# Routing choice on the logits, gate weights off GpSimd, the single tile first, and the first units' order, in a mixture-of-experts and time-mix layer

## The reference, cut to what matters

```python
xn = layernorm(x)                                # x: (2, 2048, 256), so 4096 tokens
out = x + attn(xn) + ffn(xn)

# ffn: 8 experts, 2 for each token, and a shared expert
logits = xt @ gate_w.T + gate_b                  # (4096, 8)
scores = softmax(logits)
top_w, top_i = top_k(scores, 2)
gate_dense = sum(one_hot(top_i, 8) * top_w[..., None], axis=1)
h = silu(xt @ w1e.T + b1e) * (xt @ w3e.T + b3e)  # each expert, 256 wide
y = einsum(h @ w2e.T + b2e, gate_dense)
z = silu(xt @ ws1.T + bs1) * (xt @ ws3.T + bs3) @ ws2.T + bs2   # shared, 512 wide

# attn: k, v and r from xn, a scan over time (wkv), then (sigmoid(r) * wkv) @ out_w.T
```

## Time and profile before

| | |
|---|---|
| median of 3 runs | 487.76 us (485.83 to 487.76) |
| the profiled execution | 489.11 us, its span 487.4 us |
| mean granted TensorE clock | 0.951 |
| TensorE busy | 435.8 us (89% of the span) |
| VectorE busy | 382.1 us (78%) |
| ScalarE busy | 227.1 us (47%) |
| GpSimd busy | 265.7 us (55%) |
| route / run_experts / mix, roughly | 0 to 75.5, 75.5 to 274, 274 to 487 us |

### The profile page before, as it was taken

One profiled execution on the slowest core, in us unless ns is written; L12 is line 12 of the kernel. 1 busy time (PEld: TensorE's weight loads), 2 busy tenths in 40 slices (PEclk: granted clock), 3 DMA queues, 4 the chain that ended last, 5 costly groups with the idle time before them and its releaser, 6 DMA issues.

```text
span 487.4 us, 8291 instructions
## 1 busy us (share of the span) xinstructions
PE 435.8 (89%) x2522; PEld 367.0 (75%) x2522; DVE 382.1 (78%) x707; ACT 227.1 (47%) x365; POOL 265.7 (55%) x237
## 2 busy tenths in 40 slices
PE   0896064989999999999999998999999999999997
PEld 0442053778988889888888776989898989898987
DVE  7896996876788698886966478897887969696953
ACT  1445342675876858678485543141323242414131
POOL 5005988746285865859846587837262645445000
PEclk9999555799999999999999998999999999999999
DMA  5879994326567485342454692352626170705001
GB/s 177 259 253 279 304 236 97 96 80 197 209 228 250 120 270 182 133 169 91 154 144 168 213 346 69 113 200 87 195 76 206 36 244 21 258 2 174 11 33 45
DMA packets 46242, 78.27 MB, mean 161 GB/s; under 512 B 5788, under 2 KB 32132, under 8 KB 46204
## 3 DMA queue, kind: packets, MB, share of 16 engines
q1 hardware_dynamic: 37388, 55.85, 33.5%
q0 software_dynamic: 8816, 21.93, 17.4%
HBM read 49.55 MB, written 28.21 MB: 160 GB/s over the span
## 4 chain that ended last, share of the span: by engine, by line
PE 69%; DVE 8%; POOL 8%; issue 6%; DMA 5%; SPq 1%; ACT 1%; POOLq 0%; DVEq 0%; ACTq 0%
PE ps_g L971 15%; PE ps_y L971 7%; PE ps_w L1429 6%; PE ps_w L1431 5%; PE ps_w L1430 5%; PE ps_w L1495 5%; PE ps_w L1496 5%; PE ps_w L1494 5%; DMA w_lo<-w_all 4%; POOL xg L893 3%; PE ps_x L965 3%; PE ps_h L991 2%; POOL w_lo L367 2%; PE ps_v L1429 1%; PE ps_v L1431 1%
## 5 line engine op out<-in xcount | busy, mean ns | idle before, releaser
L893 POOL DMA_INDIRECT xg<-xn_rows,tile_tok x71 | 72.4, 1020 | 30.0 <-issue 17.1
L1398 POOL DMA_INDIRECT yg<-expert_rows,rows x64 | 66.2, 1034 | 23.6 <-issue 17.1
L971 PE MATMUL ps_g<-w_hi,x_hi 128*128 x142 | 57.3, 404 | 2.3 <-DVE w_lo L380 1.7
L971 PE MATMUL ps_g<-w_lo,x_hi 128*128 x142 | 57.0, 402 | 0.0
L971 PE MATMUL ps_g<-w_hi,x_lo 128*128 x142 | 56.8, 400 | 0.0
L1429 PE MATMUL ps_w<-col_hi,s_hi 128*128 128x512 f32 x128 | 50.4, 393 | 0.2 <-DVE shid L1641 0.2
L1431 PE MATMUL ps_w<-col_hi,s_lo 128*128 128x512 f32 x128 | 50.1, 392 | 0.0
L1430 PE MATMUL ps_w<-col_lo,s_hi 128*128 128x512 f32 x128 | 50.1, 392 | 0.0
L1536 ACT ACTIVATE sact<-ps_w,vec_b 128x512 f32<-128x512 f32 x32 | 22.0, 687 | 57.5 <-PE ps_w L1431 57.5
L1406 POOL TENSOR_TENSOR col_lo<-col,col_hi 128x1024 fp32r<-128x1024 f32 x7 | 20.0, 2861 | 49.8 <-ACT col_hi L1518 49.8
L1134 DVE TENSOR_TENSOR hid<-ps_g,act 128x512 f32<-128x512 f32 (+1 forms) x36 | 23.7, 660 | 26.4 <-ACT act L1046 26.2
(11 more groups left out here) (214 smaller groups left out, 1261.6 us busy)
## 6 DMA issues: line engine op xcount, KB each, us to landing
expert_rows<-y SPq DMA_DIRECT2D x35, 256.0 KB, 2.3
w_lo<-w_all SPq DMA_DIRECT2D x16, 384.0 KB, 11.6
table<-mix_tables SPq DMA_DIRECT2D x8, 768.0 KB, 7.5
xin<-x SPq DMA_DIRECT2D x16, 256.0 KB, 3.0
xn_rows<-xn SPq DMA_DIRECT2D x16, 256.0 KB, 3.4
xn_columns<-xT SPq DMA_DIRECT2D x8, 512.0 KB, 3.7
col<-xn_columns SPq DMA_DIRECT2D x8, 512.0 KB, 6.0
res<-x SPq DMA_DIRECT2D x16, 256.0 KB, 3.5
```

What stands on the lines that cost most here:

```text
L893: pool.indirect_dma_start(out=xg[b][:, t, :], out_offset=None, in_=xn_d[:, :], in_offset=bass.IndirectOffsetOnAxis(ap=tile_tok[:, 2 * a + ...
L971: mm = nc.tensor.matmul(out, x[:, k, :], w[:, ds(e, 1), k, cols].rearrange("p o n -> p (o n)"), start=(k == 0 and n == 0), stop=(last and ...
L1398: pool.indirect_dma_start(out=yg[a.buf(2)][:, k, q, :], out_offset=None, in_=y_d[:, :], in_offset=bass.IndirectOffsetOnAxis(ap=picked[a.bu ...
```

## The change

In `choose`, both experts are found on the logits less their maximum, so that the maximum is zero: the first comparison is with zero, the winner is pushed down by -3e38 and the next maximum (`behind`) is found among what is left. `exps` is no longer waited for there. The softmax's sum, reciprocal and product move to a new function `share` that follows each `choose`; the gates are the reciprocal, and exp(behind) times it (ScalarE takes the exponential). `dense` is made by VectorE between the last one-hot batch and `tile_tok`, its rounded copies in `terms` by ScalarE, its low part by VectorE after `tile_tok` and after four `split_lo`.

GpSimd issues ten additions in route. The other six follow gathers 2, 3 and 4 in run_experts, two after each. HIGH and LOW are 10 and 4.

Unit 0 has one tile and all others have two. The order of ScalarE and VectorE in the first units is changed. The low part of `col` is cut by VectorE in the last unit, and in mix the low part of x is cut by VectorE, and the experts' first addition in step 0 is put off to its end.

```diff
-        HIGH, LOW = 12, 1
+        HIGH, LOW = 10, 4
...
             pool.wait_ge(s_xn, NSTEP - 1)
-            for i in range(8):
-                less_first(pool, i)
-
-            pool.wait_ge(s_mask, 3)
-            nc.gpsimd.tensor_tensor(dense[:], score, mask[:].rearrange("p e j -> p j e"), ALU.mult
...
-            for i in range(8, E * KC):
+            for i in range(HIGH):
                 less_first(pool, i)
...
+            act.wait_ge(s_second, 2)
+            nc.scalar.activation(gates[:, 1, :], behind[:], ACT.Exp).then_inc(s_gate, 1)
+            for i in range(HIGH - 2):
+                split(i)
+            act.wait_ge(s_terms, 3)
+            for n in (0, 2):
+                ins = nc.scalar.activation(terms[:, :, n * E:(n + 1) * E].bitcast(F32R), dense[:], ACT.Copy)
+            ins.then_inc(s_terms, 1)
+            for i in range(HIGH - 2, HIGH):
                 split(i)
...
+                own.link(nc.vector.scalar_tensor_tensor(
+                    out=work2[:, t], in0=work[:, t], scalar=0.0,
+                    in1=desc[:, None, :].broadcast_to([P, count, E]), op0=ALU.is_equal, op1=ALU.mult))
+                own.link(nc.vector.tensor_reduce(red[:, t], work2[:, t], AX_X, ALU.max))
+                own.link(nc.vector.tensor_tensor(hot[0][:, t], work2[:, t], wide(red[:, t]), ALU.is_equal))
+                own.link(nc.vector.scalar_tensor_tensor(out=left[:, t], in0=hot[0][:, t], scalar=-3e38,
+                                                        in1=work[:, t], op0=ALU.mult, op1=ALU.add))
+                nc.vector.tensor_reduce(behind[:, t], left[:, t], AX_X, ALU.max).then_inc(s_second, 1)
+                dve.wait_ge(s_second, n + 1)
...
+            def share(n, first_step, last_step):
...
                 dve.wait_ge(s_exp, n + 1)
                 own.link(nc.vector.tensor_reduce(red[:, t], score[:, t], AX_X, ALU.add))
+                own.link(nc.vector.reciprocal(gates[:, 0, t], red[:, t]))
+                own.mark(nc.vector.tensor_tensor(score[:, t], score[:, t],
+                                                 gates[:, 0, t][:, :, None].broadcast_to([P, count, E]), ALU.mult))
...
             choose(0, 0, EARLY)
+            share(0, 0, EARLY)
             for n in range(EARLY, NSTEP):
                 take(At(0, n, NSTEP))
             choose(1, EARLY, NSTEP)
-            for i in range(LOW):
-                split(i)
+            share(1, EARLY, NSTEP)
...
+            dve.wait_ge(s_terms, 2)
+            nc.vector.tensor_tensor(dense[:], score, mask[:].rearrange("p e j -> p j e"), ALU.mult
+                                    ).then_inc(s_terms, 1)
+            dve.wait_ge(s_gate, 1)
+            nc.vector.tensor_tensor(gates[:, 1, :], gates[:, 1, :], gates[:, 0, :], ALU.mult)
             dve.wait_ge(s_hotmm, PAIRS // BATCH)
...
+            for i in range(LOW):
+                split_lo(dve, i)
+            dve.wait_ge(s_terms, 4)
+            nc.vector.tensor_tensor(terms[:, :, E:2 * E], dense[:], terms[:, :, 0:E], ALU.subtract
+                                    ).then_inc(s_terms, 1)
...
-            return min(2, TILES - 2 * a)
+            return 1 if a == 0 else 2
+
+        def first_tile(a):
+            return max(0, 2 * a - 1)
...
             for a in range(AHEAD):
                 gather(a)
+                if 2 <= a < 5:
+                    for i in range(HIGH + 2 * a - 4, HIGH + 2 * a - 2):
+                        less_first(pool, i)
...
-            cut(1, col)
...
-                if a < E // 2:
-                    pe.wait_ge(s_wlo, 2 * KC * (a + 1))
+                if first_tile(a) < E:
+                    pe.wait_ge(s_wlo, KC * min(E, first_tile(a) + tiles(a)))
...
+            cut_x(0)
+            cut_x(1)
+            silu(0)
             split_hi(act, HIGH)
+            cut_x(2)
             split_hi(act, HIGH + 1)
...
                 silu(a + 1)
                 cut_h(a)
                 cut_x(a + 3)
+                if a < 2:
+                    for i in range(HIGH + 2 + 2 * a, HIGH + 4 + 2 * a):
+                        split_hi(act, i)
+                if a == 0:
+                    halves(0)
                 if r == 1 and v < NPIECE:
                     exps(v)
...
             for i in range(LOW, 6):
                 split_lo(dve, i)
             cut_x(0)
+            cut_x(1)
+            hidden(0)
+            grown(0)
+            for i in range(6, 8):
+                split_lo(dve, i)
+            cut_x(2)
+            for i in range(8, 10):
+                split_lo(dve, i)
             differences(0)
...
                 hidden(a + 1)
+                if a == DUOS - 1:
+                    dve.wait_ge(c_whi, 2)
+                    nc.vector.tensor_tensor(col[2][:], col[0][:], col[1][:].bitcast(F32), ALU.subtract
+                                            ).then_inc(c_wlo, 1)
                 cut_h(a)
                 cut_x(a + 3)
-                if a == 0:
-                    for i in range(12, E * KC - 1):
+                if a < 3:
+                    for i in range(10 + 2 * a, 12 + 2 * a):
                         split_lo(dve, i)
-                if a == 1:
-                    split_lo(dve, E * KC - 1)
...
                 if left > 0:
-                    cut(a.plus(1))
                     gather(a.plus(1))
...
+            def cut_x(a):
+                dve.wait_ge(b_xhi, a.i)
+                at_least(dve, b_z, a.i * KS - KS)
+                nc.vector.tensor_tensor(x_lo[a.buf(2)][:], xT[a.buf(2)][:], x_hi[a.buf(2)][:].bitcast(F32),
+                                        ALU.subtract).then_inc(b_xlo, 1)
...
                 if first:
                     hidden(a, 1)
+                    cut_x(a.plus(1))
                 receive(a)
-                if first:
-                    experts(a, 0)
-                elif second:
+                if second:
                     hidden(a, 0)
-                else:
+                elif not first:
                     add_outputs(a.plus(-1))
                 cut_a(a)
+                if left > 0 and not first:
+                    cut_x(a.plus(1))
...
                 if first:
-                    for g in range(1, TOPK * 2):
+                    for g in range(TOPK * 2):
                         experts(a, g)
```

More of the change, by code:

```diff
@@ new lines, in choose @@
+                dve.wait_ge(s_second, n + 1)
+                own.link(nc.vector.tensor_tensor(work2[:, t], left[:, t], wide(behind[:, t]), ALU.is_equal))
+                own.link(nc.vector.tensor_tensor(work2[:, t], work2[:, t],
+                                                 desc[:, None, :].broadcast_to([P, count, E]), ALU.mult))
+                own.link(nc.vector.tensor_reduce(red[:, t], work2[:, t], AX_X, ALU.max))
+                own.link(nc.vector.tensor_tensor(hot[1][:, t], work2[:, t], wide(red[:, t]), ALU.is_equal))
@@ L650, in choose @@
+                nc.vector.tensor_tensor(mask[:].rearrange("p e j -> p j e")[:, t], hot[0][:, t], hot[1][:, t],
+                                        ALU.add).then_inc(s_mask, 1)
+            def share(n, first_step, last_step):
+                t = slice(first_step * Q, last_step * Q)
+                count = (last_step - first_step) * Q
                 dve.wait_ge(s_exp, n + 1)
                 own.link(nc.vector.tensor_reduce(red[:, t], score[:, t], AX_X, ALU.add))
-                own.link(nc.vector.reciprocal(red2[:, t], red[:, t]))
@@ L653, in choose @@
-                own.link(nc.vector.tensor_tensor(score[:, t], score[:, t], wide(red2[:, t]), ALU.mult))
-                cur = score
-                for k in range(TOPK):
-                    own.link(nc.vector.tensor_reduce(gates[:, k, t], cur[:, t], AX_X, ALU.max))
-                    own.link(nc.vector.tensor_tensor(work2[:, t], cur[:, t], wide(gates[:, k, t]), ALU.is_equal))
-                    own.link(nc.vector.tensor_tensor(work2[:, t], work2[:, t],
-                                                     desc[:, None, :].broadcast_to([P, count, E]), ALU.mult))
-                    own.link(nc.vector.tensor_reduce(red[:, t], work2[:, t], AX_X, ALU.max))
-                    own.link(nc.vector.tensor_tensor(hot[k][:, t], work2[:, t], wide(red[:, t]), ALU.is_equal))
-                    if k == 0:
-                        own.link(nc.vector.scalar_tensor_tensor(out=work[:, t], in0=hot[0][:, t], scalar=-2.0,
-                                                                in1=score[:, t], op0=ALU.mult, op1=ALU.add))
-                        cur = work
@@ L762, in run_experts @@
         s_tok, s_xout, s_terms, s_Tout, s_wlo, (HIGH, LOW), route_parts = placed
-        split_hi, split_lo, store_columns = route_parts
+        split_hi, split_lo, store_columns, less_first = route_parts
         raw_vr, col0 = vr[0], col[0]
@@ L960, in turn_x @@
             def turn_x(a):
-                pe.wait_ge(c_gath[a % NG], a // NG * 32 + tiles(a) * 16)
+                pe.wait_ge(c_gath[a % NG], sum(tiles(u) for u in range(a % NG, a + 1, NG)) * 16)
```

(12 more changed lines are left out.)

46 lines of the change are left out of this document (13 added, 33 removed).

## The result

| | before | after |
|---|---|---|
| median of 4 runs each, same chip | 487.53 us (485.83 to 487.76) | 493.99 us (493.19 to 495.31) |
| ratio | | 1.0113, 95% interval [1.0068, 1.0157] |
| profiled execution, its span | 489.11, 487.4 us | 493.19, 491.5 us |
| mean granted clock | 0.951 | 0.948 |
| TensorE / VectorE / GpSimd busy | 435.8 / 382.1 / 265.7 us | 438.6 / 376.7 / 241.0 us |

The forecast was 486.3 us, in 482.5 to 490.2. The kernel is 1.1% slower and lies outside the range. The profiled executions differ by 4.1 us (before's is slower than each of its four runs, after's is the fastest of its four), the medians by 6.5.

The account below looks back on a forecast made before the run. TensorE, 435.8 of 487.4 us busy, loses time in route, from `s_tok` to up(3), and at mix's start. Terms +0.2 + 1.6 + 0.75 - 4.0 = -1.5 us gave 486.3 us, range 482.5 to 490.2.

Parts of the forecast that it names:

- Route: Up to `s_tok`: shorter choice saves 2.8 us, gates without GpSimd's `dense` 2.6 us; `s_tok` at 70.1 instead of 75.51.
- the last rival of C: Route: the long scan isn't GpSimd's doing, `s_tok` 1.8 us later, +0.3 us, 488.1; chance 0.05.
- Up(0) to up(2): First units of run_experts: up(0) at 79.4 instead of 86.73, up(2) at 88.6 after 1.3 us of wait.
- The weights' low parts: First units: TensorE waits for low parts, up(3) at 97.5, up(4) at 106.8; +0.2 us at the last up.
- my chain: First units: from addition 15's landing at 96.6, ScalarE reaches silu(3) at 102.4, then up(4) at 106.8.
- Rival B: First units: ScalarE waits for late additions landing in 7.5 us, up(4) at 111, +2.8 us, 490.5; chance 0.17.
- The clock: First units: two waits above 2.7 us bring half clock; the first loss hides behind silu(3), the second costs +1.6 us.
- The gathers beside splits: First units: gathers overlapping VectorE's splits issue slower, every addition up to 1.5 us later; 0.5 us taken into the landings.
- The end of run_experts: Last unit: 1.4 us of wait ahead of down(35), mix 6.9 us after the last up instead of 6.15, +0.75 us.
- The start of mix: Values(1) no longer waits for `col_lo`; outputs(0) 23.4 us after mix starts instead of 27.45, -4.0 us; other steps zero.

Follow-up runs that it names:

- e2: The changed kernel with all 16 additions issued in route again; 508.59 us, 1.0287 of the kernel before.
- e5: Changed kernel, twelve additions in route, two each behind gather(2) and gather(3), VectorE's last splits one unit ahead, exps(0) behind silu(3); 503.50 us, 1.0117 of before.
- e9: e5 with gather(4) issued ahead of additions 14 and 15 instead of behind them; 1.0010 of the kernel before.
- e12: e9 with the first experts' addition of step 0 back ahead of a_lo; 0.9944 of the kernel before.
- e3: The changed kernel with ScalarE's exps(0) moved from unit 1 to unit 2, behind silu(3); 1.0151 of the kernel before.
- e4: The changed kernel with VectorE's splits 10 to 13 in unit 0 and 14, 15 in unit 1; 1.0148 of the kernel before.
- e10: The kernel before with the changed route and mix, run_experts as before, all sixteen additions in route; 0.9984 of the kernel before.

## Why the prediction was wrong

- **Route: right.** `tile_tok` at 69.90 (70.1), the scan of L693 at 0.17 us, so GpSimd's `dense` had held it; the last rival of C is out.
- **Up(0) to up(2): right** within 0.6 us, with the wait of 1.00 us for w_lo (1.3).
- **The weights' low parts: here it failed.** I wrote "additions 12 and 13 go out at 83 and 85" and let ScalarE have the last one at 96.6. The step that failed is the time that GpSimd needs for each issue. Additions 12 and 13 went out at 85.09 and 87.60, 2.1 and 2.6 us late: the gathers began 0.6 us after 70.1, the five ahead took 1.8 us more than I had (8.04 us from the first's start to the next issue, not 6.25; 0.5 of it was in my 83), and addition 12 took 2.20 us instead of 1.55. From addition 13 to 14 it was 6.58 us, not 1.84 + 2.5: another 2.2, most of it in the second half of gather(4), 2.65 us instead of 0.95. So the last addition, which I had at 96.6 - 5.7 = 90.9, went out at 96.06, and landed 0.4 us quicker than I had it: ScalarE had it 4.8 us late, at 101.36. Behind the landing my chain was right: 10.1 us from ScalarE's last split to up(4), where I had 102.4 + 4.4 - 96.6 = 10.2. So up(4) came at 111.50 instead of 106.8, **+4.7 us**, and nothing gave it back. How much of it the order of the lists would have kept is open: in e2, without a late addition, up(4) comes 29.9 us after up(0), in the change 32.6, by my sum 27.4.
- **A wait that I left out, and that cost little here.** I counted TensorE "done with down(0) at 93.2" and never asked when gather(4) lands. It stands behind additions in the same list, and turn_x(4) waited 3.89 us. Most of that lay beside the wait for the low parts. ScalarE's and VectorE's timelines of after:

```profile
95.15 0.57 ACT L1064 ACTIVATE act<-ps_g 128x512 f32<-128x512 f32 x1
```
```profile
97.49 0.69 DVE L1145 TENSOR_TENSOR x_lo<-ps_x,x_hi 128x512 fp32r<-128x512 f32 x1 [0.44 <-ACT x_hi L1056]
98.09 1.81 DVE L382 TENSOR_TENSOR w_lo<-w_lo,w_hi 128x768 fp32r<-128x768 f32 x2
```

  Silu(2), behind the split of addition 13, came at 95.15 instead of 93.2, and with it hidden(2) and splits 12 and 13; the late gather added the 0.44 us ahead of x_lo(4). Neither moved up(4), since silu(3) waited for ScalarE's list and not for up(3). The gather counts where the additions are no longer late: it is the bound in e5 (5.69 us), and moving it ahead brings up(3) to 95.86 (e9).
- **Rival B** had the place right (ScalarE waits for late additions, up(4) at 111), and not the reason: I made it out of landings of 7.5 us, and these took 5.3. Its 0.17 was too little: GpSimd issues in order, so that every issue that takes longer delays all behind it and such errors only add up.
- **The clock: right.** One loss ahead of up(4) counts: half clock in 111.5 to 114.2 for six matmuls. From up(4) to up(5) it takes 6.58 us and later units 5.11, so it cost 1.5 (1.6 in the sum). I read one row wrongly: in the earlier trace rows work starts at 294.86 and the half clock near 296.1, 1.2 us later and not half a microsecond; nothing in the sum hangs on it. The Trainium skill ("TensorE: Matmul & The Clock Gate", HAM oscillation) says that waits between groups can bring the slow clock back again and again; the trace agrees, half clock in 100 to 104 and in 111.5 to 114.2.
- **The gathers beside splits: above the upper bound.** The first two took 1.79 and 1.40 us while VectorE split (69.81 to 73.36), the third 0.95 beside another split, the fourth 1.43, the fifth, with no split beside it, 0.95. That is 1.8 us over the five; I had 1.5 at most and took 0.5. The Trainium skill ("SBUF — State Buffer", Who interferes with whom) infers that a tensor_tensor doesn't hold the writing of descriptors, by which it would be none; the measurement decides on the time. That the splits cause it is not shown, since the third gather wasn't held and no run takes only the splits away.
- **The end of run_experts: right.** The wait ahead of down(35) was 1.29 us (1.4), and mix started 170.4 us after up(4); my terms give 277.15 - 106.8 = 170.35.
- **The start of mix: right.** -3.85 (-4.0). Without the addition that no longer waits for a gather it is 27.45 again (e12). The prediction named it, but put it second behind the early cut. Later 0.7 us of idle time came back, where I had zero.
- With 111.50 in place of 106.8 my sum gives -1.5 + 4.7 = +3.2; the mix's 0.15 and 0.7 make +4.1, the difference of the profiled executions.

## What to carry to other kernels

Where transfers of two kinds share one queue, write down the issue time of every one to the last, with the rows' longest durations and not the shortest, and ask of each kind what waits for it: the additions made a gather late, which cost 0.4 us in the change and bounded up(3) in e5, once the rest was mended. The order in the lists was worth more than the work taken off the engines: the same parts with gather(4) ahead of the last additions, splits one unit ahead and `exps` behind the silu went from 1.024 (chip B) to 1.001 (chip C) of the kernel before where mix shows the loss, and to 0.983 where it doesn't (chip D). Where two engines' lists both delay one event, an edit of either alone shows a small part of what it is worth (e3, e4); try them together before giving either up.

## What was unexpected of the hardware

- Indirect DMAs that add took 5.3 us to land when the weights' loads were over, but GpSimd was held at their issue: single additions took 4.16 and 5.74 us of GpSimd instead of 1.55 (e2, e10), single gathers 2.65 and 4.39 instead of 0.95 (after, e5). That GpSimd waited there for room in its queue is my reading; no run shows it by itself.
- One and the same kernel took 186 us and 200 us from outputs(0) to the end on two chips, through waits of up to 5.9 us that the profile puts down to nothing in the kernel. A comparison of two kernels on one chip includes such a loss, so that the change measured 1.011 on one chip and 1.024 on another.
